# Head sums turned on VectorE and carried to the projection by DMA, in a two-block vision tower

## Chip, cores and metric

The kernel runs on one core of one Trainium2 chip, as one launch. Times are microseconds on the device. Of the kernel before there are three timed runs and one profiled execution.

## What is computed

Input is x, 8 images of 32 x 32 places with 29 features. Two transformer blocks of width 128 run one after the other, each attention and then a mixture of 8 experts of which 2 are used. The change touches only the first attention with its embedding:

```python
h = x.reshape(8, 1024, 29) @ W + pe                      # tok
y = layernorm(h)
Q, K, V = y @ Wq.T + bq, y @ Wk.T + bk, y @ Wv.T + bv    # (8, 1024, 128)
Q, K, V = (t.reshape(8 * 8, 1024, 16) for t in (Q, K, V))
attn = softmax(Q @ K.T * 16 ** -0.5)
context = (attn @ V).reshape(8, 1024, 128)
out = context @ Wo.T + bo + y
h = h + layernorm(out) * gamma + beta
```

The reshape is a plain one: a "head" here is a run of 128 tokens, and its 1024 positions are (token, sixteenth of the width). So a head of a batch has 128 tokens, each cut into 8 slices j of 16 columns.

## The kernel before

`tower` runs six stages. The first is `embed_and_attend`; it handles 8 batches of 1024 tokens, and while the attention of batch b runs, the embedding, layer norm and Q, K, V of batch b + 1 are worked out between its steps. The loop over batches is written out, every engine has its own order of work by hand, and semaphores tie them together.

**Bursts.** A batch has 64 units: 4 pairs of heads x 2 halves of the queries x 8 slices of keys. TensorE computes the scores of a unit (`scores`, L426, into one of three PSUM buffers psS), ScalarE takes the exponential (L343, 128 x 1024), and TensorE multiplies by v (`weigh`, L438), adding up in psO over the slices. Two units are a burst, so a batch has 32 bursts, m = 0 to 31, and a pair of heads 8 of them. In a burst TensorE waits for two exponentials, issues scores of units 2m + 3 and 2m + 4, then weigh of units 2m and 2m + 1, and then at most one step that uses the PSUM bank psA.

**Steps through psA.** `STEPS` says in which burst each of twelve embedding steps of the next batch runs: E (token product), T (four transposes), q, k (three products each, in split precision), N (squared norms for the overflow guard), v. After TensorE's part DVE reads psA (`embed_read`, which frees the bank) and then works on (`embed_rest`, `embed_apply`). Three more bursts per pair belong to the pair before: in the second burst of a pair (r = 1) `turn`, four transposes of o_sb; DVE divides by the sums (`divide`); in the third `turn_back`, two transposes, and DVE copies them (`evacuate`); in the fourth `project`, two products with Wo, and DVE adds the input (`add_input`). The copy of psO to o_sb (`out_of_psum`, L643) is DVE's first act in the last burst of a pair (r = 7); weigh of the next pair waits for it.

**Finishing.** `UPPER` and `LOWER` place the five parts of the rest (add_bias, normal, moments, second, score) for the second half of the previous batch's tokens and the first half of this one's. Roots are taken by POOL (`root_embed`, `root_finish`), and `normal` is followed by POOL's `stream` (L295, L297, L299).

**q and k.** DVE writes their high and low parts into `parts`; SP stores them to DRAM (L209), waits until that has landed, and loads them in six transfers (L215) into the stacked operands qs and ks: `redistribute`, four times per batch. In the first batch ScalarE's queue does k's.

**Guard.** After the N steps DVE works out `unsafe`. In burst RESCUE = 26 TensorE reads its value and branches (`rescue`); in burst 25 DVE does (`guard`). With these inputs the branch that is taken sets gparts to zero. SP sends gparts into four rows of qs (`send_guard`, L238), and the first scores of a batch wait for these rows and for all loads of qs and ks (`stack_in`).

Of the kernel before, what the change touches and what calls it, by code (L numbers as in the profile page):

```python
# [7 lines left out]
F32 = mybir.dt.float32  # L8
# [98 lines left out]

def embed_and_attend(nc, H, ident, half, mean1, rstd1, score1, ins, B, S, D, NH):
# [20 lines left out]
    def score_buffer(u):  # L129
# [13 lines left out]
    PSA_PAIR, PSA_EMBED = 3, len(STEPS)  # L143
    PSA_BATCH = PSA_PAIR * HP + PSA_EMBED

    with ExitStack() as ctx:
# [28 lines left out]
        o_sb = c.sb("o_sb", [P, CH])  # L175
        stage = c.sb("stage", [P, HP * P], F32R)
        rden = c.sb("rden", [P, 4, 4])
        ctx_tm, ctxT = c.sb("ctx_tm", [P, 2, KT, DH]), c.sb("ctxT", [D, 2, P])
        res = [c.sb(f"res{p}", [P, TPC, D]) for p in range(2)]
        dq = [nc.dram_tensor(f"qparts{p}", [D, 2, 2, HALF], F32).ap() for p in range(2)]  # L180
        dk = [nc.dram_tensor(f"kparts{p}", [D, 2, 2, HALF], F32).ap() for p in range(2)]

# [4 lines left out]
         psA_free, cleared, normal_done, stream_done, qparts_done, kparts_done, qparts_out, kparts_out, stack_in, pre_qk, pre_max, gt_ps,  # L187
         gparts_done, guard_in, qk_done, exp_done, pv_done, o_evac, ht_ps, ctx_done, ct_ps, ctxT_done, staged,
         op_done, sq_done, n_ps, waited, qf_done, kf_done, unsafe_done) = (c.sem(n) for n in (
            "tok_in pe_in w_in wsplit x_in0 x_in1 emb_ps var_e root_e var_f root_f n0_done nt_ps nt_done q_ps k_ps v_ps "  # L190
            "psA_free cleared normal_done stream_done qparts_done kparts_done qparts_out kparts_out stack_in pre_qk pre_max gt_ps "
            "gparts_done guard_in qk_done exp_done pv_done o_evac ht_ps ctx_done ct_ps ctxT_done staged "
            "op_done sq_done n_ps waited qf_done kf_done unsafe_done").split())

        x_in = (x_in0, x_in1)
        N_W = 12
        STACK = 16 * 2 * 2 * len(PIECES) * CPB
# [7 lines left out]
        def redistribute(eng, b, par, kind, ch):  # L205
# [3 lines left out]
            eng.dma_start(dram[ch], parts[kind][:, :, :, :].bitcast(F32)).then_inc(out, 16)  # L209
            eng.wait_ge(out, (b * CPB + ch) * 16 + 32)  # L210
            src = dram[ch].rearrange("(j d) a p t -> d j a p t", d=DH)
            for p in range(2):
                for piece in PIECES:
                    rows = slice(64 * p + piece[2], 64 * p + piece[2] + DH)
                    eng.dma_start((qs, ks)[kind][par][rows, :, ch * HALF:(ch + 1) * HALF].bitcast(F32),  # L215
                                  src[:, :, piece[kind], p, :]).then_inc(stack_in, 16)
# [11 lines left out]
        def _(sp):  # L228
# [3 lines left out]
            def send_guard(b, par):  # L232

                sp.wait_ge(gparts_done, b + 1)
                for p in range(2):
                    for i in range(2):
                        row = 64 * p + KQ + i
                        sp.dma_start(qs[par][row:row + 1, :, :].bitcast(F32).rearrange("o j (h t) -> o (j h) t", t=P),  # L238
                                     gparts[32 * p:32 * p + 32, i, :].bitcast(F32)).then_inc(guard_in, 16)

            def batch(b, par, prior, more):
                if more:
                    if b + 2 < B:

                        sp.wait_ge(emb_ps, (b + 1) * CPB)
                        load_x(b + 2, par)
                    for ch in range(CPB):
                        for kind in range(2):
                            redistribute(sp, b + 1, 1 - par, kind, ch)
                    send_guard(b + 1, 1 - par)  # L250
# [14 lines left out]
            for ch in range(CPB):  # L265
# [1645 lines left out]
```

## Time and profile before

| | us |
|---|---|
| median of 3 runs | 1641.43 |
| lowest, highest | 1638.70, 1645.34 |
| profiled execution, device time | 1635.83 |
| its span | 1634.0 |
| its mean granted clock of TensorE | 0.873 |

| engine | busy us | share of the span |
|---|---|---|
| TensorE (PE) | 1281.6 | 78% |
| VectorE (DVE) | 1030.9 | 63% |
| ScalarE (ACT) | 1016.2 | 62% |
| GpSimd (POOL) | 526.5 | 32% |

The stage that is changed lasts from 0 to 686 us of the span; its exponentials run from 60 to 666. A line of the profile names engine, source line and operation, then the tiles as written <- read, then times. In a timeline the first two numbers are start and duration in us, and the brackets hold how long the engine stood idle before and what released it. PEclk is the granted clock of TensorE, 1.00 for 2.4 GHz and 0.50 for 1.2 GHz.

### The profile page before, as it was taken

To read this page: it belongs to the slowest core of one execution; us is meant where nothing else is said; L and a number is where in the kernel's file an instruction comes from. 1 tells how busy PE (TensorE), PEld (TensorE's weight loads), DVE (VectorE), ACT (ScalarE), POOL (GpSimd) and SP (SyncE) were. 2 spreads that over 40 slices of the span, in tenths; PEclk is the share of its full clock that TensorE was granted. 3 is DMA by queue.
4 is the path that set the end of the run, shared out by engine and by line. 5 is a ranking of instruction groups with operands and counts; after the bars stand their busy time and mean duration, and the time that the engine had idled before them with its cause. 6 is when DMAs were issued, how large, how long until landed. Compare 5 with 4: busy or idle time off the path is not lost. (4 is left out here: it accounts for less than half of the span.)

```text
span 1634.0 us, 31526 instructions
## 1 busy us (share of the span) xinstructions
PE 1281.6 (78%) x9689; PEld 843.2 (52%) x9689; DVE 1030.9 (63%) x2828; ACT 1016.2 (62%) x1358; POOL 526.5 (32%) x453
## 2 busy tenths in 40 slices
PE   3699998999998999369999948667762299999950
PEld 2344444444444444147777736556552177777740
DVE  5255756566666653437888757666653389899944
ACT  0487777787788789218888834323320188888840
POOL 3212222222221211200000011555544347667665
PEclk8699999999999999779999968667765599999985
DMA  3451606061615240011111000000010445555519
GB/s 90 80 116 21 123 13 130 19 119 27 112 38 96 55 78 2 9 35 45 39 39 46 7 11 1 30 33 31 33 34 26 143 136 147 143 152 156 147 47 308
DMA packets 134467, 118.99 MB, mean 73 GB/s; under 512 B 30459, under 2 KB 112310, under 8 KB 134350
## 3 DMA queue, kind: packets, MB, share of 16 engines
q1 hardware_dynamic: 114798, 93.75, 25.0%
q0 software_dynamic: 9216, 16.94, 3.1%
q10 hardware_dynamic: 10336, 6.82, 1.8%
q8 instruction: 64, 1.05, 0.3%
q14 instruction: 53, 0.43, 0.1%
HBM read 76.63 MB, written 42.37 MB: 73 GB/s over the span
## 5 line engine op out<-in xcount | busy, mean ns | idle before, releaser
L343 ACT ACTIVATE a_probs<-a_psS 128x1024 f32<-128x1024 f32 x512 | 491.1, 1031 | 123.3 <-PE a_psS L426 96.9
L438 PE MATMUL a_psO<-a_probs,a_v 128*32 128x256 f32 x4096 | 281.8, 394 | 24.7 <-DVE a_o_sb L643 24.1
L807 ACT ACTIVATE f_g_hi<-f_psH,f_b_hid 128x512 fp32r<-128x512 f32 x288 | 200.6, 697 | 55.4 <-PE f_psH L71 47.5
L922 DVE TENSOR_TENSOR f_g_lo<-f_g,f_g_hi 128x512 fp32r<-128x512 f32 x288 | 197.7, 688 | 53.3 <-ACT f_g L809 51.2
L1738 POOL DMA_INDIRECT result<-f_out,f_idx x160 | 186.5, 1166 | 114.8 <-issue 57.6
L426 PE MATMUL a_psS<-a_qs,a_ks 50*128 50x512 f32 x1024 | 193.1, 456 | 25.1 <-issue 12.4
L809 ACT ACTIVATE f_g<-f_psH,f_b_hid 128x512 f32<-128x512 f32 x288 | 199.7, 694 | 0.0
L438 PEld LDWEIGHTS a_psO<-a_probs,a_v 128*32 128x32 f32 x4096 | 108.5, 111 | 169.5 <-issue 88.5
L1164 POOL DMA_INDIRECT queue<-all_row,all_idx x128 | 127.0, 992 | 102.8 <-DVEq L1554 47.2
L1249 POOL TENSOR_TENSOR a_rs<-a_veps,all_half 128x8 f32<-128x8 f32 x16 | 26.6, 1662 | 337.5 <-DVE a_veps L83 337.4
L426 PEld LDWEIGHTS a_psS<-a_qs,a_ks 50*128 50x128 f32 x1024 | 78.9, 190 | 97.8 <-ACT a_probs L343 47.3
L69 PE MATMUL f_psH<-f_x_hi,f_w_lo 128*128 128x512 f32 x288 | 125.3, 435 | 2.8 <-DVE f_w_lo L64 2.6
L69 PE MATMUL f_psY<-f_g_hi,f_w_lo 128*128 128x512 f32 x288 | 116.8, 405 | 8.3 <-DVE f_w_lo L64 6.3
L71 PE MATMUL f_psH<-f_x_hi,f_w_hi 128*128 128x512 f32 x288 | 115.4, 401 | 0.0
L70 PE MATMUL f_psH<-f_x_lo,f_w_hi 128*128 128x512 f32 x288 | 115.2, 400 | 0.0
L71 PE MATMUL f_psY<-f_g_hi,f_w_hi 128*128 128x512 f32 x288 | 113.5, 394 | 0.0
L70 PE MATMUL f_psY<-f_g_lo,f_w_hi 128*128 128x512 f32 x288 | 113.0, 392 | 0.0
L279 POOL TENSOR_TENSOR a_rs_f<-a_veps_f,all_half 128x4 f32<-128x4 f32 x32 | 32.4, 1012 | 168.7 <-DVE a_veps_f L98 168.7
L64 DVE TENSOR_TENSOR f_w_lo<-f_raw,f_w_hi 128x512 fp32r<-128x512 f32 x112 | 77.5, 692 | 8.4
L1399 PE MATMUL a_psO<-a_diag,a_v 128*128 128x128 f32 x128 | 29.3, 421 | 59.1 <-DVE a_diag L1503 59.1
L817 ACT ACTIVATE f_x_hi<-f_psX 128x512 fp32r<-128x512 f32 x56 | 33.6, 600 | 66.8 <-PE f_psX L845 66.8
L69 PEld LDWEIGHTS f_psY<-f_g_hi,f_w_lo 128*128 128x128 f32 x288 | 54.0, 188 | 34.5 <-issue 17.9
(289 smaller groups left out, 2235.1 us busy)
## 6 DMA issues: line engine op xcount, KB each, us to landing
f_raw<-W SPq DMA_DIRECT2D x80, 256.0 KB
a_qs<-qparts SPq DMA_DIRECT2D x96, 128.0 KB, 4.6
a_ks<-kparts SPq DMA_DIRECT2D x84, 128.0 KB, 4.5
f_rows<-queue SPq DMA_DIRECT2D x40, 260.0 KB, 2.6
qparts<-a_parts SPq DMA_DIRECT2D x16, 512.0 KB, 2.6
f_raw<-w SPq DMA_DIRECT2D x32, 256.0 KB, 2.6
kparts<-a_parts SPq DMA_DIRECT2D x14, 512.0 KB, 3.3
out_y<-result SPq DMA_DIRECT2D x8, 512.0 KB, 11.4
```

The source lines that it names most:

```text
L64: return nc.vector.tensor_tensor(lo, src, hi.bitcast(F32), ALU.subtract)
L69: nc.tensor.matmul(out, w_lo, x_hi, start=first, stop=False)
L70: nc.tensor.matmul(out, w_hi, x_lo, start=False, stop=False)
L71: return nc.tensor.matmul(out, w_hi, x_hi, start=False, stop=last)
L343: nc.scalar.activation(probs[u % NPR][:, :], psS[score_buffer(u)][:, :, :].rearrange("p a n -> p (a n)"), ACT.Exp).then_inc(exp_done, 1)
L426: last = nc.tensor.matmul(psS[score_buffer(u)][:, p, :], ks[par][64 * p:64 * p + KG, kt, hp * P:(hp + 1) * P], queries(par, hp, p, a), sta ...
L438: last = nc.tensor.matmul(psO[32 * g:32 * g + 32, a * HALF:(a + 1) * HALF], v[par][:, 2 * hp + p, kt, :], probs[u % NPR][:, cols:cols + HA ...
L807: nc.scalar.activation(g_hi[i][:, n, :], psH[n][:, :], ACT.Gelu, bias=b_hid[i][:, n:n + 1])
L809: nc.scalar.activation(g[:, n, :], psH[n][:, :], ACT.Gelu, bias=b_hid[i][:, n:n + 1]).then_inc(g_done, 1)
L922: nc.vector.tensor_tensor(g_lo[i][:, n, :], g[:, n, :], g_hi[i][:, n, :].bitcast(F32), ALU.subtract).then_inc(lo_done, 1)
L1164: pool.indirect_dma_start(queue, bass.IndirectOffsetOnAxis(ap=idx[:, k, t:t + 1], axis=0), rows[:, t, :], None).then_inc(sent, 16)
L1738: pool.indirect_dma_start(result, bass.IndirectOffsetOnAxis(ap=idx[i][:, j:j + 1], axis=0), out[i][:, j, :], None, bounds_check=2 * B * S ...
```

## The change

- `out_of_psum` is now DVE's 32x32 block transpose of psO into o_t: tokens come to lie on partitions within blocks of 32. `divide` takes reciprocals of the sums there, multiplies in place and transposes the blocks back into o_n. It runs in the first burst of the next pair.
- `turn`, `turn_back` and `evacuate` are gone. SP stores o_n in four transfers to a DRAM tensor (`spread`), waits until they have landed, and loads it as ctxT in one transfer.
- `project` and `add_input` move from the fourth burst of a pair to the last (r = 7).
- STEPS, UPPER, LOWER and APPLY are laid out anew. RESCUE goes from 26 to 24, so DVE's guard from burst 25 to 23. Three parts of the first half of a batch's tokens (moments, second, score) move into the next batch.
- `stack_in` becomes two semaphores, one for each half of the loads; the second is waited for at unit 32. In the first batch POOL's queue sends the guard rows.
- `clear` sets only the columns of v that no step writes, to 1.

```diff
-    STEPS = {0: ("E", 0), 4: ("E", 1), 6: ("T", 0), 8: ("q", 0), 12: ("k", 0), 14: ("T", 1), 16: ("q", 1), 20: ("k", 1),
-             22: ("N", 0), 24: ("N", 1), 28: ("v", 0), 30: ("v", 1)}
+    STEPS = {1: ("E", 0), 3: ("E", 1), 5: ("T", 0), 9: ("q", 0), 11: ("k", 0), 13: ("T", 1), 17: ("q", 1), 19: ("k", 1),
+             20: ("N", 0), 22: ("N", 1), 28: ("v", 0), 30: ("v", 1)}
-    TURN, BACK, PROJECT = 1, 2, 3
-    RESCUE = 26
+    PROJECT = 7
+    RESCUE = 24
-    UPPER = {3: "add_bias", 7: "normal", 10: "moments", 11: "second", 13: "score"}
-    LOWER = {21: "add_bias", 23: "normal", 26: "moments", 27: "second", 29: "score"}
-    APPLY = {1: 0, 5: 1}
+    UPPER = {2: ("moments", 0), 4: ("second", 0), 6: ("score", 0), 10: ("add_bias", 1), 12: ("normal", 1), 18: ("moments", 1), 20: ("second", 1),
+             25: ("score", 1)}
+    LOWER = {27: ("add_bias", 0), 29: ("normal", 0)}
+    APPLY = {2: 0, 8: 1}
...
+            def spread(pair):
+
+                sp.wait_ge(norm_done, pair + 1)
+                for p in range(2):
+                    for cc in range(2):
+                        row = 64 * p + 32 * cc
+                        sp.dma_start(dctx[64 * cc:64 * cc + 64, p, :].rearrange("(i d) t -> d i t", d=DH),
+                                     o_n[row:row + DH, :].rearrange("d (i t) -> d i t", t=P)).then_inc(ctx_out, 16)
+                sp.wait_ge(ctx_out, (pair + 1) * 4 * 16)
+                if pair:
+                    sp.wait_ge(op_done, pair)
+                sp.dma_start(ctxT[:, :, :], dctx).then_inc(ctx_in, 16)
 
             def batch(b, par, prior, more):
+                if prior:
+                    spread(b * HP - 1)
+                if b + 2 < B:
+
+                    sp.wait_ge(emb_ps, (b + 1) * CPB)
+                    load_x(b + 2, par)
+                for q in range(CPB):
+                    spread(b * HP + q)
+                    if more:
+                        redistribute(sp, b + 1, 1 - par, 0, q)
+                        redistribute(sp, b + 1, 1 - par, 1, q)
                 if more:
...
+                    send_guard(sp, b + 1, 1 - par)
+                spread(b * HP + 2)
...
             for kind, ch in FIRST:
                 embed_step(kind, ch, 0)
+            send_guard(pool, 0, 0)
             pool.drain()
             clear(1)
...
+                if u % (UNITS // CPB) == 0:
+                    pe.wait_ge(stack_in[u // (UNITS // CPB)], (b + 1) * STACK)
                 if u == 0:
-                    pe.wait_ge(stack_in, (b + 1) * STACK)
-                    pe.wait_ge(guard_in, (b + 1) * GUARD)
+                    wait_guard(pe, b)
...
             def out_of_psum(b, hp):
                 dve.wait_ge(pv_done, b * UNITS + ((hp + 1) * UPP + NPR))
-                nc.vector.tensor_copy(o_sb[:, :], psO[:, :]).then_inc(o_evac, 1)
+                nc.vector.transpose(o_t[:, :, :].rearrange("p k e -> p (k e)"), psO[:, :]).then_inc(o_evac, 1)
 
             def divide(pair):
-                dve.wait_ge(ht_ps, pair + 1)
...
+                dve.drain()
+                nc.vector.reciprocal(rden[:, :].unsqueeze(2), o_t[:, :, DH:DH + 1])
+                dve.drain()
+                nc.vector.tensor_tensor(o_t[:, :, 0:DH], o_t[:, :, 0:DH], rden[:, :].unsqueeze(2).broadcast_to([P, CH // 32, DH]), ALU.mult)
+                dve.drain()
+                if pair:
+                    dve.wait_ge(ctx_out, pair * 4 * 16)
+                nc.vector.transpose(o_n[:, :], o_t[:, :, :].rearrange("p k e -> p (k e)")).then_inc(norm_done, 1)
```

## Rows read from the trace of the kernel before

**Rows 1.** The page's costliest groups: x count | busy us, mean ns | idle before, releaser.

```profile
L343 ACT ACTIVATE a_probs<-a_psS 128x1024 f32<-128x1024 f32 x512 | 491.1, 1031 | 123.3 <-PE a_psS L426 96.9
...
L1164 POOL DMA_INDIRECT queue<-all_row,all_idx x128 | 127.0, 992 | 102.8 <-DVEq L1554 47.2
...
L279 POOL TENSOR_TENSOR a_rs_f<-a_veps_f,all_half 128x4 f32<-128x4 f32 x32 | 32.4, 1012 | 168.7 <-DVE a_veps_f L98 168.7
```

**Rows 2.** Stretches, second and seventh batch: length, busy us, then PEclk, DMA share, GB/s.

```profile
140.41:219.27 78.86, 72.67 (x740) 35.36 (x737) 49.52 (x139) 61.60 (x65) 17.88 (x16) 0.96 0.38 71
...
529.99:605.68 75.69, 69.59 (x740) 34.32 (x736) 49.28 (x139) 61.40 (x65) 18.31 (x16) 1.00 0.39 72
```

**Rows 3.** Timeline of TensorE, sixth batch, bursts 1 to 5 and 8.

```profile
456.95 0.73 PE L426 MATMUL a_psS<-a_qs,a_ks 50*128 50x512 f32 x4
...
459.20 0.73 PE L426 MATMUL a_psS<-a_qs,a_ks 50*128 50x512 f32 x4
...
461.23 0.73 PE L426 MATMUL a_psS<-a_qs,a_ks 50*128 50x512 f32 x4
...
463.54 0.73 PE L426 MATMUL a_psS<-a_qs,a_ks 50*128 50x512 f32 x4
...
466.29 0.73 PE L426 MATMUL a_psS<-a_qs,a_ks 50*128 50x512 f32 x4
...
467.95 0.73 PE L426 MATMUL a_psS<-a_qs,a_ks 50*128 50x512 f32 x4
...
473.92 1.07 PE L438 MATMUL a_psO<-a_probs,a_v 128*32 128x256 f32 x16 [1.33 <-DVE a_o_sb L643]
```

**Rows 4.** Timeline of DVE, sixth batch: an E step, a T step, the copy.

```profile
457.06 0.69 DVE L513 TENSOR_TENSOR all_H<-a_psA,a_pe_tab 128x512 f32<-128x512 f32 x1 [2.25 <-PE a_psA L358]
...
459.24 0.17 DVE L98 TENSOR_SCALAR a_veps_e<-a_mv_e 128x4 f32<-128x4 f32 x1
...
471.29 0.69 DVE L517 COPY a_nT<-a_psA 128x512 f32<-128x512 f32 x1
...
473.18 0.68 DVE L643 COPY a_o_sb<-a_psO 128x512 f32<-128x512 f32 x1
...
473.96 1.12 DVE L104 TENSOR_SCALAR a_res<-a_res,a_mv_f,a_rs_f 128x128 f32<-128x128 f32 x4
```

**Rows 5.** Timeline of DVE and TensorE, second batch, before burst 26.

```profile
203.39 0.14 DVE L566 TENSOR_SCALAR a_unsafe<-a_bound 1x1 int32<-1x1 f32 x1
...
204.58 0.73 PE L426 MATMUL a_psS<-a_qs,a_ks 50*128 50x512 f32 x4 [1.69 <-issue]
```

**Rows 6.** Groups by line: a block transpose, two subtractions or sums, POOL's stream.

```profile
L1503 DVE STREAM_TRANSPOSE a_diag<-a_pr 32x256 f32<-32x256 f32 x32 | 14.0, 436 | 1.7 <-issue 1.2
...
L554 DVE TENSOR_TENSOR a_parts<-a_kf,a_parts 128x512 fp32r<-128x512 f32 x16 | 24.8, 1552 | 1.8 <-issue 0.5
...
L295 POOL TENSOR_TENSOR a_res<-a_res,a_brow 128x512 f32<-128x512 f32 x16 | 20.5, 1282 | 53.5 <-DVE a_res L104 53.5
...
L580 DVE TENSOR_TENSOR a_res<-a_res,a_brow 128x512 f32<-128x512 f32 x16 | 11.1, 693 | 1.5
```

**Rows 7.** Timeline of SP's queue, third batch: six loads of a stack.

```profile
276.72 2.68 SPq L215 DMA_DIRECT2D a_ks<-kparts  x6
```

**Rows 8.** From issue to landing, by line: first the stores L209, then L215's loads.

```profile
DMA to landing us min/median/max: 2.6/3.2/7.8
...
DMA to landing us min/median/max: 3.0/4.7/9.2
```

**Rows 9.** Timeline of the head of the stage: guard rows issued, first scores.

```profile
48.81 2.55 SPq L238 DMA_DIRECT2D a_qs<-a_gparts  x4
...
59.61 1.65 PE L426 MATMUL a_psS<-a_qs,a_ks 50*128 50x512 f32 x6 [10.35 <-DMA a_qs<-a_gparts]
```

**Rows 10.** Timeline of DVE after the last weigh.

```profile
667.18 0.69 DVE L643 COPY a_o_sb<-a_psO 128x512 f32<-128x512 f32 x1 [2.56 <-PE a_psO L438]
...
671.41 0.42 DVE L664 TENSOR_TENSOR a_res<-a_psA,a_n 128x256 f32<-128x256 f32 x1 [0.91 <-PE a_psA L458]
```

More of the change, by code:

```diff
@@ L105, in standardise, with moments @@
     return last
+def moments(nc, dve, src, stat, mv, veps, var_done, tiles=TPC):
+    for i in range(tiles):
+        nc.vector.bn_stats(stat[:, i, :], src(i))
+    dve.drain()
+    for i in range(tiles):
+        nc.vector.bn_aggr(mv[:, i, :], stat[:, i, :])
+    dve.drain()
+    nc.vector.tensor_scalar(veps[:, :], mv[:, :, 1], EPS, None, ALU.add).then_inc(var_done, 1)
+def standardise(nc, src, dst, mv, rs, tiles=TPC):
+    for i in range(tiles):
+        last = nc.vector.tensor_scalar(dst(i), src(i), mv[:, i, 0:1], rs[:, i:i + 1], ALU.subtract, ALU.mult)
+    return last
 def embed_and_attend(nc, H, ident, half, mean1, rstd1, score1, ins, B, S, D, NH):
@@ L264, in _ @@
             sp.wait_ge(cleared, 2)
-            for ch in range(CPB):
-                redistribute(sp, 0, 0, 0, ch)
-            send_guard(0, 0)
+            redistribute(sp, 0, 0, 0, 0)
+            redistribute(sp, 0, 0, 0, 1)
             sp.wait_ge(cleared, 4)
             rounds(batch)
+            spread(B * HP - 1)
         @block.gpsimd
@@ L333, in _ @@
             rounds(batch)
-            for part in UPPER.values():
-                finish(part, B - 1, 1)
+            for part, half_ in UPPER.values():
+                finish(part, B - 1, half_)
         @block.scalar
@@ L440, in weigh @@
                 last.then_inc(pv_done, 1)
-            def turn(pair):
-                pe.wait_ge(o_evac, pair + 2)
-                for i in range(4):
-                    last = nc.tensor.transpose(psA[:, i * P:(i + 1) * P], o_sb[:, i * P:(i + 1) * P], ident[:, :])
-                last.then_inc(ht_ps, 1)
-            def turn_back(pair):
-                pe.wait_ge(ctx_done, pair + 1)
-                for p in range(2):
-                    last = nc.tensor.transpose(psA[:, p * P:(p + 1) * P], ctx_tm[:, p, :, :].rearrange("p j d -> p (j d)"), ident[:, :])
-                last.then_inc(ct_ps, 1)
             def project(pair):
-                pe.wait_ge(ctxT_done, pair + 1)
+                pe.wait_ge(ctx_in, (pair + 1) * 16)
                 for p in range(2):
@@ L477, in batch @@
                         embed_step(*STEPS[m], b + 1, 1 - par, psA[:, :])
-                    if r in (TURN, BACK, PROJECT) and (q or prior):
+                    if r == PROJECT and pair >= 0:
                         pe.wait_ge(psA_free, uses.next())
-                        {TURN: turn, BACK: turn_back, PROJECT: project}[r](pair)
+                        project(pair)
             pe.sem_inc(pv_done, NPR)
@@ L495, in _ @@
             uses = Tally((B - 1) * PSA_BATCH - PSA_PAIR + PSA_PAIR * HP)
-            for step in (turn, turn_back, project):
-                pe.wait_ge(psA_free, uses.next())
-                step(B * HP - 1)
+            pe.wait_ge(psA_free, uses.next())
+            project(B * HP - 1)
         @block.vector
@@ L673, in batch @@
                         embed_read(*STEPS[m], b + 1, 1 - par, psA[:, :], True)
-                    if q or prior:
-                        pair, hp = b * HP + (q - 1), (q - 1) % HP
-                        if r == TURN:
-                            divide(pair)
-                        elif r == BACK:
-                            evacuate(pair)
-                        elif r == PROJECT:
-                            add_input(pair, par if q else 1 - par, hp)
+                    if r == BPP - 1 and (q or prior):
+                        add_input(b * HP + (q - 1), par if q else 1 - par, (q - 1) % HP)
+                    if r == 0 and (q or prior):
+                        divide(b * HP + (q - 1))
                     if more and m in STEPS:
@@ L716, in _ @@
             divide(out)
-            evacuate(out)
-            add_input(out, (B - 1) % 2, HP - 1)
-            for part in UPPER.values():
-                finish(part, B - 1, 1)
+            for part, half_ in UPPER.values():
+                if (part, half_) == ("add_bias", 1):
+                    add_input(out, (B - 1) % 2, HP - 1)
+                finish(part, B - 1, half_)
 def rank(nc, dve, out, more, same, p, lower):
```

86 lines of the change are left out of this document (42 added, 44 removed).

## Prediction

> **What bounds the kernel now.** I read the engines' groups first: the exponentials (L343) are busy for 491 us and stand idle for 123 us, and what they wait for is TensorE, nearly always its scores (L426) [rows 1]. So in the first stage ScalarE is the floor and TensorE's order of work is what ends last. Second, the stretches by batch: from 140.41 to 605.68 (529.99 + 75.69) six like batches take 465.3 us, 77.5 each [rows 2]; the first runs up to 140.41, the last has no embedding of a next one beside it. Third, TensorE's timeline: each burst of two units begins with scores, so the distance between two starts of L426 is the length of a burst. With a turn it is 2.25 us, with a turn back 2.03, with a projection 2.31, with an embedding product 2.75, with nothing beside it 1.66 [rows 3]. A burst with nothing is paced by two exponentials, at most 1.92 us (491.1 / 512 twice) [rows 1], once TensorE has caught up. A T burst has the four transposes of a turn, 2.25; a q or k burst lies between, about 2.55.
>
> By these lengths a batch of before is 4 x (2.25 + 2.03 + 2.31) + 8 x 1.66 = 39.6 us plus 29.5 for the twelve embedding bursts (four of 2.75, two of 2.25, four of 2.55, two short ones of about 1.86), together 69.1. Measured are 77.5: 8.4 us of a batch are waits. Two kinds are visible. weigh waits for the copy out of psO because DVE is late with a T step: 1.33 us [rows 3], DVE being in L517 to L545 until 473.18 [rows 4]. And before burst 26 TensorE waits for `unsafe` and reads it: it is written at 203.39 + 0.14, scores begin at 204.58, 1.05 us later and 1.69 us after the last product [rows 5]. Where such waits fall, the granted clock falls too: 0.96 in the second batch, 1.00 in the seventh, which is 3.2 us shorter [rows 2].
>
> **Work taken off TensorE.** Four turns and four turns back per batch go. Eight bursts of 2.25 and 2.03 become bursts of 1.66: 4 x (0.59 + 0.37) = 3.8 us. Bursts 25 to 27 now have nothing beside them, so the exponentials pace them, up to 0.26 us each above 1.66; I take 0.45 in all. New work per batch: 65.7 us, 3.4 less. In the last batch only the projection is left in burst 7 of each pair: a burst with nothing there already costs near the exponentials' pace, so I take 0.65 per pair, 2.6 us.
>
> **Work on DVE.** Per pair the copy out of psO (0.68 [rows 4]) becomes a 128x512 block transpose. The row of L1503 is 0.436 us for 256 columns [rows 6]: the bounds are 0.69 (as the copy) and 0.87 (twice the row); I take 0.71, since part of a short instruction is fixed. The source in PSUM is not shown by any row. Then a reciprocal, a product and a second transpose, all in SBUF, about 1.6 us with drains, replace reciprocal, product and copy, about 1.1. That is 0.5 us more DVE per pair, beside other work, with nobody on TensorE waiting for it at once: the result is wanted seven bursts later. Cover gone, it would cost its 0.5 us per pair, 16 us.
>
> **Is DVE on time at psO?** I count from the end of burst 1's E product. DVE: E block 2.35 [rows 4], root on POOL 1.0 [rows 1] and its gap, four scalings 1.12 [rows 4] (4.7), moments of the lower half, now moved to burst 2, 1.8 (6.5), second E block (8.9), `second` 1.3 (10.2), T block 1.9 (12.1), `score`, two of 0.69 (13.7), transpose (14.4). TensorE: 1.66 + 2.75 + 1.66 + 2.25 + 1.66 + 1.66 = 11.6, projection 0.65 and scores 0.66: at 12.95 weigh of burst 8 wants psO. Stall 1.5 us. In burst 16: `normal` of the upper half in burst 12 releases POOL's three operations of 1.3 us each (L295 and two more) [rows 6]; T's cast and subtraction come beside them. With blocking, DVE is free at 31.0 and its transpose ends at 31.7, weigh wants psO at 30.7: 1.0 us. Without it, none. The row for blocking: L554, a subtraction whose inputs are both in SBUF, takes 1.55 us right beside POOL's square, while L580, the same size with no POOL work beside it, takes 0.69 [rows 6]. I take 1.0.
>
> The Trainium skill, page "SBUF — State Buffer", section "SBUF: two separate sides", says that DVE with two SBUF inputs and a GpSimd operation that reads SBUF hold a shared port pair exclusively, the later one blocking. L554 agrees. By that rule burst 16 keeps its 1.0 us; if the rule did not reach this pair of operations, the six batches would be 6 us shorter in all.
>
> At bursts 24 and 0 DVE has done by then and the projection in burst 23 or 31 hides the transpose. If the transpose were 0.87, stalls grow by 0.16 at two places.
>
> **The guard, moved from 26 to 24.** The sequence N step, DVE's chain, value read keeps its distance of two bursts, but POOL's stream no longer lies in it and no turn does. TensorE arrives with `unsafe` just written; the 1.05 us of reading it stay [rows 5], with 0.1 of lateness 1.15 us. The rewriting of psO, 0.7 us, lies under it. So 3.65 us of waits (1.5, 1.0, 1.15) remain, plus 1.2 for clock falls (between 0 and the 3 that [rows 2] show).
>
> **The SP queue.** This is the new resource. `spread` is four stores of 32 KB (0.45 us to issue each, as L215's 2.68 / 6 [rows 7]), a wait for them, one load. No row has such a store; the nearest is qparts, 16 times larger: 2.6 us to landing at best, median 3.2, at most 7.8 [rows 8]. I take 2.4 for the landing, 5 in all to the load's issue, 7.3 to ctxT. On the same scale as above: pair 0's divide ends at 16.7, its load is issued at 21.4; q0's store goes then (its parts are ready at 21.1), six loads until 26.9, k0's store waits behind them (5 us; the loads take 4.7 to land, median [rows 8]), its loads until 34.7, pair 1's spread until 39.5, where q1's parts have been ready for 1 us; q1 until 45.4, k1 until 53.1, the guard's four (2.55 [rows 9]) until 55.7 and landed at 58.2. Scores of the next batch want it in burst 30, at 59.9: 1.7 us of slack. Pair 2's ctxT lands at 62.5 and is wanted in burst 31 at 64.3. Waits behind them: q0's, k0's, q1's, k1's stacks, then the guard, and all of TensorE behind that. I take 0.5 us per batch, bounds 0 and 4. The second halves of the stacks are now waited for only at unit 32, half a batch later, so they are free. The loads of x come early and cost nothing. `divide` also waits for the stores of the pair before, and SP for its projection, before ctxT is overwritten: both are a pair's length old, about 18 us.
>
> **Sum per like batch**: 65.7 + 3.65 + 1.2 + 0.5 = 71.05 against 77.5: 6.5 x 6 = 39.0 us. First batch: no part of an earlier batch is finished in it, so its handoffs are on time; it saves the 3.4 of work and about 4.6 of waits, 8.0. Last: 2.6.
>
> **Head.** TensorE stands for 10.35 us until the guard rows land; SP issued them at 48.81, behind its loads, over 2.55 us [rows 9]. Now POOL issues them from 46.3 on, in its own queue; 0.99 us each by L1164 [rows 1], so until 50.3, and landing 2.6 to 7.8 us later [rows 8]: 52.9 to 58.1, against 59.6. Scores no longer wait for the loads of the second half. I take 54.1, 5.5 us. POOL's clearing of the second buffers moves behind these four issues; the first root that it delays is wanted after burst 1, so nothing. Cover gone: if POOL's transfers queue behind the loads after all, 0.
>
> **Tail.** Before, from the copy at 667.18 to the last add_input at 671.41 it takes 4.2 us [rows 10]. After: transpose and divide 2.4, four stores issued 1.8 to 2.6, landing 2.4, load 0.45 + 2.4, projection 0.7, about 11.2 us. DVE does `moments`, `second` and `score` of the lower half meanwhile, about 5.7 us. Cost 7.0, bounds 5 and 12.
>
> **Total**: -39.0 - 8.0 - 2.6 - 5.5 + 7.0 = -48.1 us. The profiled execution took 1635.8 us (span 1634.0), so 1587.7 there; the median of the runs is 5.6 above it, so 1593.
>
> **Rivals.** (1) Fuller gain: DVE is not late at bursts 8 and 16 and the clock holds. Then the 1.5, 1.0, 1.2 and 0.5 go, 4.2 x 6 = 25: 1568. For it: in the seventh batch the clock is 1.00 throughout. Against: the sums of DVE's chain. (2) DVE becomes late at more handoffs, because the transpose from PSUM costs 1.2 to 1.4 (no row shows that source) or POOL blocks more: 0.6 at four handoffs and in the chain before the late ones, about 2.5 x 7 = 18: 1611. (3) Slower: the SP chain. If landings beside the loads are those of the worst rows (7.8 in place of 2.9 for q1's store and of 5 for k1's, 4.8 for 2.4 at the spread and at the guard), the guard is 12.5 us later, less 1.7 of slack and the 0.5 counted: 10.3 x 7 = 72: 1665. It decides from about 8 us per batch (57 us, which lifts the sum over the bound), that is from a chain 9.7 us later. For it: the head has such landings, with twice the queues loading. Against: in the later batches DMA is busy for 0.38 of the time [rows 2]. (4) The removed transposes hide entirely under the exponentials: excluded, since a turn burst is 0.59 longer than an empty one.
>
> **Chances.** Forecast 0.50 (1580 to 1605), fuller gain 0.15, DVE late 0.22, SP chain 0.08, a milder SP chain of 5 to 8 us per batch 0.05. A change of 0.5%, 8 us, is about what a measurement tells from none. Faster 0.87, same 0.05, slower 0.08. Range 1565 to 1625.
>
> **What would show it.** Starts of L426 1.66 apart in bursts where turns were; a wait for the psO transpose of about 1.5 us in burst 8, 1.0 in 16, none in 24 and 0; the wait before burst 24 at 1.15; like batches of about 71 us; first scores near 54; last add_input 11 us after psO's last transpose begins. Wrong it would be if scores at burst 30 wait for the guard or L458 waits for ctxT by several us, or if the block transpose from PSUM is over 0.9 us.

## Result and profile after

The changed kernel takes 1633.78 us (median of 20 runs) against 1642.82 us of the kernel before, in runs beside each other on one chip: a ratio of 0.9945, 95% interval 0.9928 to 0.9963. It is 9 us faster where 48 were forecast, and outside the range at its slow end. Its profiled execution has a span of 1629.8 us. Two runs took far longer than all others of their kernel, one of e11 (4031 us) and one of the kernel before beside e10 and e11 (1771 us): the ratios leave them out, the medians count them.

The costliest groups of the changed kernel, and three of its DMA issues (out<-in, queue, count, KB each, median us to landing), on the page:

```profile
span 1629.8 us, 31265 instructions
...
L398 ACT ACTIVATE a_probs<-a_psS 128x1024 f32<-128x1024 f32 x512 | 483.1, 1042 | 116.9 <-PE a_psS L483 64.4
...
L483 PE MATMUL a_psS<-a_qs,a_ks 50*128 50x512 f32 x1024 | 194.2, 455 | 51.3 <-DMA a_qs<-a_gparts 37.7
...
qparts<-a_parts SPq DMA_DIRECT2D x16, 512.0 KB, 2.9
kparts<-a_parts SPq DMA_DIRECT2D x14, 512.0 KB, 6.4
contexts<-a_o_n SPq DMA_DIRECT2D x128, 32.0 KB, 2.1
```

The exponentials (L398, before L343) still stand idle for 117 us, hardly less than the 123 of [rows 1]. But what stands ahead of the scores (L483) is now 37.7 us on a DMA: the guard rows, `qs` from `gparts`. The two stores of 512 KB, the same transfer by the same line, take 2.9 us to landing for q and 6.4 for k.

Three waits of TensorE from 60 to 670 us, those that this text follows (engine, what it writes, line, for whom: total us, times, longest):

```profile
PE a_psS L483 <- DMA a_qs<-a_gparts: 30.8, 7, 6.7
PE a_psO L495 <- DVE a_o_t L687: 14.5, 12, 1.8
PE a_psA L502 <- DMA a_ctxT<-contexts: 7.3, 1, 7.3
```

Seven waits of TensorE on the guard rows, one for each batch that is followed by another, 30.8 us in all. The stretches by batch (second and last: columns as in [rows 2]) say what is left of the gain:

```profile
136.08:213.76 77.68, 69.01 (x714) 33.35 (x713) 50.26 (x140) 60.65 (x65) 18.10 (x16) 0.96 0.46 85
...
594.07:649.61 55.54, 53.41 (x613) 23.02 (x612) 23.92 (x82) 54.74 (x61) 10.10 (x9) 1.00 0.09 21
```

TensorE is busy for 69.0 us of the second batch, not 72.7: the work did go. Yet six like batches take 458.0 us (136.08 to 594.07), 76.3 each, where they took 77.5. Where the rest went is seen in TensorE's timeline, around the start of burst 30 in the third batch:

```profile
278.23 0.51 PE L483 MATMUL a_psS<-a_qs,a_ks 50*128 50x512 f32 x2
...
283.40 0.80 PE L483 MATMUL a_psS<-a_qs,a_ks 50*128 50x512 f32 x2 [4.67 <-DMA a_qs<-a_gparts]
...
284.13 1.93 PE L495 MATMUL a_psO<-a_probs,a_v 128*32 128x256 f32 x16
...
285.34 1.02 ACT L398 ACTIVATE a_probs<-a_psS 128x1024 f32<-128x1024 f32 x1 [5.38 <-PE a_psO L495]
```

Two of the four scores go, the other two belong to the next batch and wait 4.67 us for its guard rows; ScalarE stands behind them. After the stand the sixteen matmuls of weigh take 1.93 us where they take 1.07 elsewhere in this trace: the clock has fallen, to 0.52 from the end of the wait to the end of the burst:

```profile
283.40:287.89 4.49, 4.49 (x26) 2.66 (x26) 0.00 (x0) 1.02 (x1) 0.00 (x0) 0.52 0.09 29
```

Burst 30 is 9.66 us long here and 11.80, 10.02, 9.66, 8.44, 7.19, 9.46 and 7.99 in the seven batches, where 2.75 is its length without a wait. The excess is 45.3 us, 30.8 of it the waits themselves; the other 14.5 I put down to work at a lower clock after them, which the granted clock shows after each of the seven.

### The profile page after: what moved, and what is told of

It reads as the page before. It is cut to its first block and busy times, and to the rows that moved or that the text cites. A ratio compares the mean times of both kernels' runs of the same rounds, so it can differ in the third digit from the quotient of the medians.

```text
span 1629.8 us, 31265 instructions
## 1 busy us (share of the span) xinstructions
PE 1267.0 (78%) x9497; PEld 835.6 (51%) x9497; DVE 1039.5 (64%) x2828; ACT 1008.9 (62%) x1358; POOL 520.9 (32%) x455
## 5 line engine op out<-in xcount | busy, mean ns | idle before, releaser
L398 ACT ACTIVATE a_probs<-a_psS 128x1024 f32<-128x1024 f32 x512 | 483.1, 1042 | 116.9 <-PE a_psS L483 64.4
L495 PE MATMUL a_psO<-a_probs,a_v 128*32 128x256 f32 x4096 | 282.3, 394 | 14.8 <-DVE a_o_t L687 14.5
L483 PE MATMUL a_psS<-a_qs,a_ks 50*128 50x512 f32 x1024 | 194.2, 455 | 51.3 <-DMA a_qs<-a_gparts 37.7
L1774 POOL DMA_INDIRECT result<-f_out,f_idx x160 | 181.5, 1134 | 121.3 <-DVEq L1798 67.4
L483 PEld LDWEIGHTS a_psS<-a_qs,a_ks 50*128 50x128 f32 x1024 | 79.3, 189 | 141.9 <-issue 71.0
L64 DVE TENSOR_TENSOR f_w_lo<-f_raw,f_w_hi 128x512 fp32r<-128x512 f32 x112 | 77.5, 692 | 8.3
```

The costliest lines, as they stand in the source:

```text
L64: return nc.vector.tensor_tensor(lo, src, hi.bitcast(F32), ALU.subtract)
L398: nc.scalar.activation(probs[u % NPR][:, :], psS[score_buffer(u)][:, :, :].rearrange("p a n -> p (a n)"), ACT.Exp).then_inc(exp_done, 1)
L483: last = nc.tensor.matmul(psS[score_buffer(u)][:, p, :], ks[par][64 * p:64 * p + KG, kt, hp * P:(hp + 1) * P], queries(par, hp, p, a), sta ...
L495: last = nc.tensor.matmul(psO[32 * g:32 * g + 32, a * HALF:(a + 1) * HALF], v[par][:, 2 * hp + p, kt, :], probs[u % NPR][:, cols:cols + HA ...
L1774: pool.indirect_dma_start(result, bass.IndirectOffsetOnAxis(ap=idx[i][:, j:j + 1], axis=0), out[i][:, j, :], None, bounds_check=2 * B * S ...
```

## The SP queue, link by link

SP's queue in that third batch, with what the prediction had for each link. The table counts from 218.17, the end of burst 1's E product, as the prediction does; its last row is the start of the scores that wait for the guard:

```profile
234.52 1.71 SPq L283 DMA_DIRECT2D contexts<-a_o_n  x4
237.50 0.34 SPq L288 DMA_DIRECT2D a_ctxT<-contexts  x1
239.23 0.34 SPq L229 DMA_DIRECT2D qparts<-a_parts  x1
241.83 2.69 SPq L239 DMA_DIRECT2D a_qs<-qparts  x6
244.69 0.34 SPq L229 DMA_DIRECT2D kparts<-a_parts  x1
251.10 2.67 SPq L239 DMA_DIRECT2D a_ks<-kparts  x6
253.81 1.85 SPq L283 DMA_DIRECT2D contexts<-a_o_n  x4
260.73 0.34 SPq L288 DMA_DIRECT2D a_ctxT<-contexts  x1
...
266.80 0.43 SPq L229 DMA_DIRECT2D kparts<-a_parts  x1
273.79 2.67 SPq L239 DMA_DIRECT2D a_ks<-kparts  x6
276.51 2.41 SPq L253 DMA_DIRECT2D a_qs<-a_gparts  x4
```

| link | forecast | measured |
|---|---|---|
| q0's six loads issued | 26.9 | 26.4 |
| wait for k0's store, which stands behind q0's loads | 5 | 6.4 |
| k0's loads issued | 34.7 | 35.6 |
| landing of pair 1's four stores, behind k0's loads | 2.4 | 5.1 |
| ctxT load of pair 1 | 39.5 | 42.6 |
| q1's loads issued | 45.4 | 48.6 |
| wait for k1's store, behind q1's loads | 5 | 7.0 |
| k1's loads issued | 53.1 | 58.3 |
| guard rows issued | 55.7 | 60.8 |
| guard rows landed, behind k1's loads | 58.2 | 65.2 |

The first links are on time, pair 0's stores among them, with nothing in front of them: 237.50 less 236.23, the end of their issue, is 1.3 us. The four later links that stand right behind six loads take 1.4, 2.7, 2.0 and 2.0 us more than I gave them, 8.1 in all. The other links came 1.1 shorter, so the guard is 7.0 us later than forecast, against a slack of 1.7.

## Experiments

All ratios are against the kernel before, in runs beside it on the same chip; "like batch" is the mean of batches 2 to 7 in the profiled execution. Of the theories, the first is the SP queue's order (the guard rows land late because they stand behind k1's loads), its rivals are the contexts' own transfers, DVE's lateness at psO and the moved rescue.

**e1: the guard rows ahead of k1's loads.**

```diff
-                        redistribute(sp, b + 1, 1 - par, 1, q)
+                        store_parts(sp, b + 1, 1, q)
+                        if q == 0:
+                            load_parts(sp, b + 1, 1 - par, 1, q)
                 if more:
                     send_guard(sp, b + 1, 1 - par)
+                    load_parts(sp, b + 1, 1 - par, 1, 1)
                 spread(b * HP + 2)
```

> In each batch SP stores k1's parts, then sends the guard rows, then loads k1's stack (which is wanted only 32 units later). Theory (the guard rows are late because they queue behind k1's six loads and behind what spread adds ahead of them): the wait of 3 to 6.7 us before burst 30's second unit is gone; the context of pair 2 now stands behind k1's loads and TensorE waits 0 to 2.5 us for it in burst 31. About 1600 us, 28 to 38 below the changed kernel. Rival A (the DMA engines themselves are too busy, the order in SP's queue is not what matters): the guard lands about as late, time within 8 us of the changed kernel, 1626 to 1642. Rival B (DVE's lateness and the clock are what is missing): also within 8 us.

1609.05 us, ratio 0.9788 (0.9764 to 0.9812). Burst 30 is 2.75 us long in all seven batches: no wait on the guard is left. In its place comes one in burst 31, which is 7.25, 3.96, 4.45, 5.15, 3.54, 3.95 and 2.80 instead of 2.31: the projection waits for ctxT, whose stores now stand right behind k1's loads. So the cause of the guard's wait is its place in the queue, and a wait moves to whoever is next in it. The new one was larger than expected in two batches (4.9 and 2.8 us, for at most 2.5), and the time is 9 us above the 1600 expected.

**e2: both second-half loads, q1's and k1's, at the end of the batch's queue**, behind the guard rows and pair 2's `spread`. They are wanted at unit 32 of the next batch.

```diff
-                        redistribute(sp, b + 1, 1 - par, 0, q)
-                        redistribute(sp, b + 1, 1 - par, 1, q)
+                        for kind in range(2):
+                            store_parts(sp, b + 1, kind, q)
+                            if q == 0:
+                                load_parts(sp, b + 1, 1 - par, kind, q)
                 if more:
                     send_guard(sp, b + 1, 1 - par)
                 spread(b * HP + 2)
+                if more:
+                    for kind in range(2):
+                        load_parts(sp, b + 1, 1 - par, kind, 1)
```

> Both loads of the second half (q1, k1) go behind the guard rows and behind pair 2's spread. Theory: no wait in burst 30 nor in burst 31; like batches of 70 to 71.5 us, 1593 to 1600 us, 34 to 40 below the changed kernel and 2 to 8 below the variant that moves k1's loads alone. Rival A: within 8 us of the changed kernel. If the second half's loads now come too late for unit 32 (burst 14), a wait on them shows there; they are issued about 25 us before that, so I expect none.

1589.77 us, ratio 0.9665 (0.9640 to 0.9690): 44 us less than the changed kernel, by the order of one queue. Its SP queue, third batch:

```profile
246.12 0.43 SPq L229 DMA_DIRECT2D qparts<-a_parts  x1
246.59 0.43 SPq L229 DMA_DIRECT2D kparts<-a_parts  x1
253.55 2.44 SPq L253 DMA_DIRECT2D a_qs<-a_gparts  x4
256.03 1.99 SPq L283 DMA_DIRECT2D contexts<-a_o_n  x4
259.29 0.34 SPq L288 DMA_DIRECT2D a_ctxT<-contexts  x1
259.68 2.81 SPq L239 DMA_DIRECT2D a_qs<-qparts  x6
262.54 4.57 SPq L239 DMA_DIRECT2D a_ks<-kparts  x6
```

Its second batch:

```profile
129.17:198.71 69.54, 65.75 (x713) 31.81 (x713) 50.29 (x140) 60.39 (x65) 18.16 (x16) 1.00 0.55 99
```

The stores of pair 2's contexts, with no loads ahead of them, need 1.3 us from the end of their issue (258.02) to the load (259.29). Bursts 30 and 31 are 2.75 and 2.31 in every batch. Like batches take 70.4 us; TensorE's busy time in the second is 3.3 us lower than in the changed kernel for the same instructions, at a clock of 1.00 instead of 0.96.

**e3: the guard rows by POOL's queue**, in burst 24 of each batch, all else as changed.

```diff
-                if more:
-                    send_guard(sp, b + 1, 1 - par)
...
+                    if more and m == RESCUE:
+                        send_guard(pool, b + 1, 1 - par)
```

> SP's order stays, but the guard rows of every batch are issued by POOL, in its own queue, as those of the first batch are already. Theory (position in SP's queue): they are issued 9 to 10 us earlier, at the time DVE has them ready, need about 4 us to issue and 3 to 5 to land, and arrive 0 to 1.5 us before or after they are wanted; wait in burst 30 at most 1.5 us, a wait of 0 to 2 us for pair 2's context in burst 31; 1598 to 1612. Rival A (busy DMA engines): they land 8 us or more after issue though nothing of their own queue is ahead, and the time stays above 1620.

1607.25 us, ratio 0.9783 (0.9755 to 0.9812), and like e1 in all: burst 30 is 2.75, burst 31 grows to 7.98, 4.48, 4.15, 4.97, 3.46, 3.21 and 4.02. The guard rows of these seven batches, from issue to landing:

```profile
DMA to landing us min/median/max: 2.7/3.7/6.6
```

They stand in a queue of their own here, while q1's loads and k1's store of SP are in flight. They take 3.7 us at the median, against 4.8 behind k1's loads in the changed kernel and 2.1 in e2, where they go out 7 us after the last store of SP. In e1, where SP issues them behind the same q1 loads and k1 store, it is 3.7 too. So with the same transfers in flight SP's queue and another one give the same landing: it is the traffic in flight that counts here as far as these runs tell, and how POOL's rows land with nothing in flight no run shows. The wait goes because the rows are issued earlier: 50.7 us after burst 1's E product for 58.3 (third batch).

**e4: no context transfers.** It leaves out the transfers of the contexts, so the projection takes `o_n` as it stands and the output is not the one asked for.

```diff
-                sp.wait_ge(norm_done, pair + 1)
-                for p in range(2):
-                    for cc in range(2):
...
-                sp.dma_start(ctxT[:, :, :], dctx).then_inc(ctx_in, 16)
...
-                pe.wait_ge(ctx_in, (pair + 1) * 16)
+                pe.wait_ge(norm_done, pair + 1)
...
-                    last = nc.tensor.matmul(psA[:, p * P:(p + 1) * P], ctxT[:, p, :], w_raw[:, 3, :], start=True, stop=True)
+                    last = nc.tensor.matmul(psA[:, p * P:(p + 1) * P], o_n[:, p * P:(p + 1) * P], w_raw[:, 3, :], start=True, stop=True)
...
-                    dve.wait_ge(ctx_out, pair * 4 * 16)
+                    dve.wait_ge(op_done, pair)
```

> Leaves out the transfers of the contexts: the projection takes o_n as it stands, so the output is not the reference's. Everything else as in the changed kernel, SP's order of q, k and guard too. Theory: without spread SP is 3 to 7 us earlier from q1 on, the guard rows land in time, burst 30 waits 0 to 1 us; the tail gets 5 to 6 us shorter as well; 1586 to 1598. It gives the price of carrying the contexts by DMA in this order, 36 to 48 us. Rival B (DVE and the clock): 5 to 8 us below the changed kernel, the tail alone.

1599.05 us, ratio 0.9738 (0.9714 to 0.9762). The waits of e1, e3 and e4, with the total, the times and the longest:

```profile
PE a_psA L505 <- DMA a_ctxT<-contexts: 21.4, 8, 7.3
```

```profile
PE a_psA L502 <- DMA a_ctxT<-contexts: 22.2, 8, 7.2
```

```profile
PE a_psS L474 <- DMA a_qs<-a_gparts: 4.3, 4, 1.5
```

One of the eight ctxT waits in e1 and in e3 is the tail's (7.3 and 7.2), which every version with transfers has. Without the contexts' transfers the guard still comes up to 1.5 us late in four batches, since it stands behind k1's loads as before. e4 is 9 us slower than e2: of the two, the order counts for more than the added traffic. The tail, expected to be 5 to 6 us shorter, is 1.0 shorter (8.5 us for 9.5 from psO's last transpose to the last add_input).

**e5 to e7: DVE at psO.** All three are e2 with one step of DVE's list placed elsewhere: `score` of the lower half from burst 6 to 8 (e5), `normal` of the upper half from burst 12 to 14 (e6), both (e7). The cut shows e7's.

```diff
-    UPPER = {2: ("moments", 0), 4: ("second", 0), 6: ("score", 0), 10: ("add_bias", 1), 12: ("normal", 1), 18: ("moments", 1), 20: ("second", 1),
+    UPPER = {2: ("moments", 0), 4: ("second", 0), 8: ("score", 0), 10: ("add_bias", 1), 14: ("normal", 1), 18: ("moments", 1), 20: ("second", 1),
```

> On top of the order with the second half's loads last (1589.8 us): `score` of the lower half goes from burst 6 to burst 8 on DVE, behind the transpose out of psO. Theory of the prediction (the wait of 1.5 us in burst 8 is DVE's chain E, apply, moments, E, second, T, score): 1.5 us leave the chain, burst 8 falls from 3.15 to 1.7, and the clock falls that follow it in some batches go too. 1.5 to 2.5 us in six batches, 9 to 15 us: 1575 to 1582. Rival (the block transpose itself or the read of psO is what weigh waits for): burst 8 stays near 3.1, time unchanged.

> On top of the same order: `normal` of the upper half goes from burst 12 to burst 14, so that POOL's three operations do not run beside the T step of burst 13. Theory (DVE's cast and its subtraction with both inputs in SBUF are held up by POOL's operations): the T block takes 1.9 us again, the wait of 0.95 us in burst 16 goes (2.62 to 1.67), 5 to 6 us in six batches: 1583 to 1586. Rival (DVE is simply late by its own work in bursts 9 to 13): `normal`'s own 1.12 us only moves within the chain ahead of the transpose out of psO in burst 15, so burst 16 keeps most of its wait and the T block was 1.9 us before as well.

> Both moves together on top of the same order. If the two waits are separate, the gains add: 14 to 21 us below 1589.8, 1569 to 1576. If the second wait only grows when the first one goes, since TensorE then comes earlier against DVE's chain, burst 16 keeps 0.5 to 1 us and the sum falls short by 3 to 6 us.

| kernel | median us | ratio (95%) | burst 8 | burst 16 |
|---|---|---|---|---|
| e2 | 1589.77 | 0.9665 (0.9640 to 0.9690) | 3.14 to 3.53 | 2.61 to 2.64 |
| e5 | 1586.76 | 0.9679 (0.9640 to 0.9717) | 1.66 to 1.98 | 3.40 to 3.54 |
| e6 | 1581.83 | 0.9630 (0.9598 to 0.9663) | 3.14 to 3.53 | 1.66 |
| e7 | 1577.76 | 0.9601 (0.9567 to 0.9636) | 1.66 to 1.99 | 2.12 to 2.49 |

e5 missed: the 1.5 us went from burst 8 and 0.8 of it came back in burst 16. TensorE comes there 1.5 us earlier, but DVE, with `score` now in this stretch and no gap left in it, begins its T step only 0.7 us earlier (fourth batch). Its interval overlaps that of e2. e6 shows what the wait in burst 16 was. DVE and POOL around psO's transpose, in the changed kernel:

```profile
245.96 1.30 POOL L349 TENSOR_TENSOR a_res<-a_res,a_brow 128x512 f32<-128x512 f32 x1 [1.84 <-DVE a_res L122]
...
246.75 0.79 DVE L586 CAST a_nT_hi<-a_nT 128x512 fp32r<-128x512 f32 x1
...
247.62 1.62 DVE L588 TENSOR_TENSOR a_nT_lo<-a_nT,a_nT_hi 128x512 fp32r<-128x512 f32 x1
249.16 0.70 DVE L687 STREAM_TRANSPOSE a_o_t<-a_psO 128x512 f32<-128x512 f32 x1
```

and in e6, where POOL's stream begins after them:

```profile
228.78 0.43 DVE L591 CAST a_nT_hi<-a_nT 128x512 fp32r<-128x512 f32 x1
229.28 0.69 DVE L593 TENSOR_TENSOR a_nT_lo<-a_nT,a_nT_hi 128x512 fp32r<-128x512 f32 x1
...
231.27 1.28 POOL L354 TENSOR_TENSOR a_res<-a_res,a_brow 128x512 f32<-128x512 f32 x1 [3.91 <-DVE a_res L122]
```

The cast falls from 0.79 to 0.43 and the subtraction from 1.62 to 0.69, and burst 16 is as short as an empty one. e7 is the fastest kernel of the study, 4.0% below the one before. Its 12.0 us below e2 are about the 3.0 and 7.9 of e5 and e6 together, but less than the two waits of 1.5 and 0.95 in six batches, 14.7, and just short of the 14 to 21 expected: 0.5 to 0.8 us of burst 16 stays.

**e8 and e11: the rescue back at 26**, in the changed kernel and in e2.

```diff
-    RESCUE = 24
+    RESCUE = 26
```

> The changed kernel with the guard back at burst 26 on TensorE and 25 on DVE, as it was before. Theory (the guard rows stand behind k1's loads in SP's queue and are issued about 58 us after burst 1, DVE having them ready at 51 in burst 23): ready at 54 to 56 from burst 25 they are still not what SP waits for, so burst 30 waits as long as in the changed kernel and the time stays within 5 us of it, 1629 to 1640; the earlier guard bought nothing in this order. Rival (the guard's own time of readiness is what is late in burst 30): 3 to 4 us more in each of seven batches, 1655 to 1662.

> The order with the second half's loads last (1589.8 us), and the guard back at burst 26 on TensorE and 25 on DVE. In this order SP waits for the guard rows themselves, so here their time of readiness should count: ready 3.5 to 4 us later, they are issued at about 55 to 57.5 us after burst 1 and land near 59.6, when scores of burst 30 want them at 59.9; pair 2's context lands at 64, wanted at 64.3. Theory: within 6 us of 1589.8, with 0 to 1 us of wait in bursts 30 or 31. If landing beside other transfers takes as long as in the changed kernel (4.8 us), burst 30 waits 2 to 3 us per batch and the time is 1604 to 1612: then the earlier guard is worth that much once the order is right.

e8: 1632.61 us, 0.9935 (0.9905 to 0.9964), burst 30 from 7.14 to 11.01. e11: 1591.3 us, 0.9623 (0.9574 to 0.9671), burst 30 at 2.75. Neither can be told from its partner (0.9945 and 0.9665). Working the guard out in burst 23 bought nothing that these runs can tell, in either order: in the changed kernel the rows wait for their turn in the queue, in e2 they have slack.

**e9 and e10: more ahead of the guard.** In e9 one copy of 512 KB from DRAM to DRAM stands ahead of the guard's four transfers, in e10 six loads of half the size of a stack's, into a tile that nobody reads.

```diff
                 if more:
+                    if b:
+                        sp.wait_ge(waste_done, b * 16)
+                    sp.dma_start(dwaste, dk[1]).then_inc(waste_done, 16)
                     send_guard(sp, b + 1, 1 - par)
```

```diff
                 if more:
+                    if b:
+                        sp.wait_ge(waste_done, b * 16 * 6)
+                    src = dk[1].rearrange("(j d) a p t -> d j a p t", d=DH)
+                    for p in range(2):
+                        for piece in PIECES:
+                            rows = slice(64 * p + piece[2], 64 * p + piece[2] + DH)
+                            sp.dma_start(waste[rows, :, :], src[:, 0:KT // 2, piece[1], p, :]).then_inc(waste_done, 16)
                     send_guard(sp, b + 1, 1 - par)
```

> The changed kernel with one more transfer in SP's queue between k1's loads and the guard rows: 512 KB copied from k's DRAM parts to a scratch tensor in DRAM. Theory (the guard is late by what stands ahead of it in its queue): the wait in burst 30 grows by 2.5 to 4 us in seven batches, 18 to 30 us: 1652 to 1664. Rival (busy DMA engines, order of no matter): SP has the queue free soon after and DMA is busy for 0.4 of the time, so 0 to 5 us.

> The changed kernel with six more loads of k's parts, half as large as k1's and like them in row length, into a scratch tile, between k1's loads and the guard rows. The 512 KB copy from DRAM to DRAM at this place had added only 0.7 us to burst 30. Theory (what counts is time in SP's queue, issue and landing, and the copy took little of both): six issues of 0.45 us alone delay the guard by 2.7 us, their landing by up to 1.5 more; burst 30 grows by 2.7 to 4.2 us in seven batches, 19 to 30 us above the changed kernel's 1633.8, and every SP step after it is as late: 1651 to 1668. Rival (the guard's landing is fixed by something other than what stands ahead of it): below 1642.

e9: 1641.41 us, 0.9976 (0.9949 to 1.0003); e10: 1648.17 us, 1.0028 (1.0004 to 1.0052). Their waits on the guard:

```profile
PE a_psS L487 <- DMA a_qs<-a_gparts: 34.5, 7, 7.7
```

```profile
PE a_psS L491 <- DMA a_qs<-a_gparts: 46.7, 7, 8.7
```

The seven bursts 30 sum to 64.6 us in the changed kernel, 69.2 in e9 and 81.6 in e10: 0.66 and 2.44 us more per batch. In e8, whose guard rows go out as in the changed kernel, they sum to 62.3, so that of the 0.66 some 0.3 may be scatter between executions. e10's queue, third batch, the six added loads and the guard's four:

```profile
282.15 4.04 SPq L310 DMA_DIRECT2D a_waste<-kparts  x6
286.24 2.41 SPq L254 DMA_DIRECT2D a_qs<-a_gparts  x4
```

Six half loads delay the guard's issue by 4.1 us and the next batch by 2.4, a little under my 2.7; the time, too, is just below the 1651 expected. e9 was a miss, since one transfer of 512 KB cost far less than expected of it. Here the price goes by what must be issued ahead, and less by bytes alone. That the batch is lengthened by less than the issue is delayed goes with a faster landing of the guard rows: 3.6 us at the median in e10 for 4.8 in the changed kernel, perhaps because k1's loads are now 4 us further ahead of them. Some 0.5 us stays open.

## Why the prediction was wrong, step by step

**The SP queue** is the step that failed: "I take 0.5 us per batch, bounds 0 and 4." The mechanism and its place were named, the chain was drawn link by link, and the size was wrong. Like batches take 76.3 us in the changed kernel and 70.4 in e2, which differs from it by the order alone: 5.9 us per like batch, and 8.9 in the first (77.46 and 68.56), together 44.5, the 44.0 us between the two medians. The wrong term was the landing of what stands right behind six loads of 128 KB: 2.4, 5 and 2.5 were taken, 5.1, 6.4 to 7.0 and 4.5 measured. The 2.4 and 2.5 lay even below the shortest landing of [rows 8], 2.6, and I did not ask what stood ahead of the transfers that make up a median. In the kernel before nothing stood right ahead of them (third batch):

```profile
266.43 2.67 SPq L215 DMA_DIRECT2D a_qs<-qparts  x6
272.99 0.34 SPq L209 DMA_DIRECT2D kparts<-a_parts  x1
...
284.07 2.95 SPq L238 DMA_DIRECT2D a_qs<-a_gparts  x4
```

The store of k1 goes out 3.9 us after q1's loads are issued (269.10), the guard 4.7 us after k1's (279.40, [rows 7]); in the changed kernel these gaps are 0.04 and 0.05 us. So the old rows could not show the new landing, and the four errors of 1.4 to 2.7 us met a slack of 1.7. It fits the milder form of the SP rival (5 to 8 us per batch), to which I gave 0.05, not the severe one. That form begins where the range ends: the range's end, 1625, is 32 us above 1593, or 4.6 more in each of seven batches, and not the 8 from which the prediction says that the rival decides. And the upper bound of 4 left out that the clock falls to 0.5 behind these waits (2.9 to 6.7 us): a third of the excess in burst 30.

**Work taken off TensorE**: right. Empty bursts are 1.66 and, three after burst 24, 1.78 to 1.83; the last batch gained 3.0 us (58.53 to 55.54) for 2.6.

**Like batches, the queue left aside**: 70.55 by the sum, 70.4 in e2. Burst 8 waits for psO's transpose by 1.5 us where the clock is full (3.13 to 3.15 against 1.66; up to 3.59), as computed; burst 16 by 0.95 for 1.0; burst 23 is longer by 1.1 to 1.6 for 1.15; bursts 24 and 0 wait for nothing. Clock falls cost about 0.9 for 1.2: three of e2's like batches are 69.4 to 69.6 us long, the other three 71.0 to 71.6. That burst 16 was blocking between DVE and POOL, for which the prediction cites the Trainium skill, page "SBUF — State Buffer", section "SBUF: two separate sides", e6 bears out with 0.79 and 1.62 against 0.43 and 0.69.

**DVE**: the block transpose out of PSUM takes 0.705 us at the median of 32 (693 to 718 ns), for 0.71. This was the ground of the rival "DVE late", which did not come.

**The guard moved**: harmless, as costed, and also of no use (e8, e11). Reading `unsafe` stayed: 1.2 us from its writing to the scores, for 1.05 before.

**Head**: POOL issues a guard row in 0.53 us, not 0.99 (L1164 is an indirect transfer, the wrong row for it), and the first scores begin at 55.70 rather than 59.61: 3.9 us for 5.5. In the twelve traces of kernels with this head they begin between 55.4 and 59.4, in e2 at 57.70; so this term moves by 4 us between executions, and the 3.9 lie near its lucky end. POOL's four rows land 3.8 to 10.9 us after their issue in these traces, for the 2.6 to 7.8 taken.

**First batch**: 9.3 us in e2 (77.89 to 68.56) for 8.0, and 0.4 in the changed kernel, where its guard wait is the longest of all.

**Tail**: longer, as said, but mostly for another reason. After psO's last copy or transpose begins it took 4.6 us to the last add_input [rows 10]; now:

```profile
652.58 0.72 DVE L687 STREAM_TRANSPOSE a_o_t<-a_psO 128x512 f32<-128x512 f32 x1 [5.39 <-PE a_psO L495]
655.28 1.71 SPq L283 DMA_DIRECT2D contexts<-a_o_n  x4
658.29 0.34 SPq L288 DMA_DIRECT2D a_ctxT<-contexts  x1
660.47 1.20 PE L502 MATMUL a_psA<-a_w_raw,a_ctxT 128*128 128x128 f32 x4 [7.31 <-DMA a_ctxT<-contexts]
661.70 0.42 DVE L702 TENSOR_TENSOR a_res<-a_psA,a_n 128x256 f32<-128x256 f32 x1 [0.94 <-PE a_psA L502]
```

9.5 us to 662.12, 4.9 more for 7.0: with nothing ahead of them the stores land in 1.3 us after their issue and the load in 2.2. But until 660.77 DVE is at the `moments`, `second` and `score` that now stand ahead of the last add_input (with 1.1 us for a root by POOL), and it waits only 0.94 us for the projection. In e4, without any transfer, the same way takes 8.5 us. So 3.9 of the 4.9 us are there with no transfer at all, by DVE's order, which the prediction took to be hidden under the transfers; these add 1.0.

**The total.** First scores, first batch, like batches, last batch and tail (4.5 us by the stage's end) of the changed kernel give 3.9 + 0.4 + 7.3 + 3.0 - 4.5 = 10.1 us: the stage's end, SP's first issue of the next stage, lies at 676.66 for 686.76. In e2 it is 1.9 + 9.3 + 42.8 + 3.0 - 4.5 = 52.6 less by the unrounded times, where the prediction without its 0.5 in six batches has 51.1. That the two are so near is in part luck: the head came 3.6 us short, the tail 2.5 and the first batch 1.3 over. But the span fell by only 4.2 us (1634.0 to 1629.8), because the stages behind, whose code is the same, took 5.9 us longer. The same stretch of the third stage, 300 to 315 us after the first stage's end, before and then after:

```profile
986.76:1001.76 15.00, 10.85 (x115) 9.16 (x116) 11.03 (x43) 7.87 (x10) 1.72 (x2) 0.85 0.00 1
```

```profile
976.66:991.66 15.00, 11.47 (x120) 11.02 (x120) 10.53 (x42) 6.80 (x9) 2.86 (x2) 0.75 0.01 1
```

The granted clock is 0.75 there, for 0.85; about 4 us are lost between 290 and 340 us behind the first stage's end. The other traces of changed kernels that I set beside it are 3 to 8 us longer behind that point too. The profiled execution of before took 1635.8 us, 7.0 below the median of its runs and 2.9 below the fastest of twenty, so a likely reading is that its later stages were luckier than those of a usual run. The differences of the medians follow the first stage's end in three kernels: 9.0 for 10.1 in the changed kernel, 52.7 for 52.6 in e2, 66.0 for 65.9 in e7 (620.88). In the other nine the two lie 0.7 to 7.2 us apart (5.4 for -1.8 in e9, 11.2 for 5.3 in e8), so this reading is not shown, nor is what decides the clock there.

## What to carry to other kernels

A queue that issues in order is a resource with a timetable: put small transfers that somebody waits for ahead of large loads that are wanted half a batch later, and give each transfer behind loads the landing that a trace shows with such loads in flight, not the median of the line. Where no row has such a place, the term is open and its bounds must say so. When the slack of a chain is smaller than the likely error of its sum, the price is what lies beyond it, a falling clock included. What is laid "under" a wait must itself end before the wait does (the tail). When one wait is removed, look who stands next in the same queue or on the same engine (e1, e3, e5).

## What was not expected of the hardware

- The same store of 512 KB lands 2.9 us after its issue with no loads right ahead of it (median of q's) and 6.4 (median of k's, up to 7.7) behind six loads of the same queue. The guard's 16 KB rows, by their line: median 4.8 us in the changed kernel, 3.7 by POOL's queue in e3, 2.1 in e2.
- A copy of 512 KB from DRAM to DRAM ahead of the guard costs a batch 0.66 us, scatter included, six loads of half a stack 2.4.
- DVE's 32x32 block transpose of 128x512 fp32 takes 0.71 us from PSUM as from SBUF, about what a plain copy takes (0.68) [rows 4].
- POOL issues a plain DMA in 0.50 to 0.79 us, an indirect one in 0.99 [rows 1].
